# Sending the tokens of seven batches to their two experts through memory, in two waves, instead of running all eight experts on every token

## The reference, cut to what matters

```python
def _L3_ffn_ref(X, We, be, Wr, br, Wo, bo):
    router_logits = jnp.einsum('bsd,ed->bse', X, Wr) + br
    router_weights = jax.nn.softmax(router_logits, axis=-1)
    top_k_weights, top_k_indices = jax.lax.top_k(router_weights, TOP_K)
    expert_outputs = jnp.einsum('bsd,ehd->bseh', X, We) + be
    gathered = jnp.take_along_axis(expert_outputs, top_k_indices[..., None], axis=2)
    combined = jnp.sum(top_k_weights[..., None] * gathered, axis=2)
    out = jnp.einsum('bsd,hd->bsh', combined, Wo) + bo
    return out
```

## Time and profile before

| | us |
|---|---|
| median of 3 runs (652.51 to 654.73) | 654.12 |
| the profiled execution's own time | 654.19 |
| its span | 652.4 |
| PE busy in the span | 570.7 (87%) |
| DVE busy | 475.4 (73%) |
| ACT busy | 300.3 (46%) |
| POOL busy | 118.6 (18%) |
| mean granted PE clock | 0.97 of 2.4 GHz |

### The profile page before, as it was taken

How to read it: one execution, slowest core, us unless ns; L and a number is a source line. 1 busy time by engine, 2 the same in 40 slices (tenths; PEclk the granted TensorE clock), 3 DMA queues, 4 the chain that set the end, 5 groups by cost and what they waited for, 6 DMA issues and landing times.

```text
span 652.4 us, 10840 instructions
## 1 busy us (share of the span) xinstructions
PE 570.7 (87%) x3994; PEld 385.1 (59%) x4032; DVE 475.4 (73%) x1273; ACT 300.3 (46%) x472; POOL 118.6 (18%) x115
## 2 busy tenths in 40 slices
PE   9884776867989989989889888999999999999897
PEld 4743433745766756757667666656575756565443
DVE  4677868857678687787876776786968778786664
ACT  2346677626555455554545554243343425253110
POOL 2121000351313313313223132103030200000000
PEclk9886899889999999999999998999999999999999
DMA  9600000574135043143143240405032140000000
GB/s 335 258 1 1 1 0 2 127 220 128 52 98 150 28 123 114 56 132 113 35 146 89 59 146 19 127 1 162 2 100 62 41 122 16 2 17 1 17 18 16
DMA packets 40636, 51.15 MB, mean 78 GB/s; under 512 B 4180, under 2 KB 33620, under 8 KB 40276
## 3 DMA queue, kind: packets, MB, share of 16 engines
q1 hardware_dynamic: 40584, 50.46, 25.8%
HBM read 35.63 MB, written 14.68 MB: 77 GB/s over the span
## 4 chain that ended last, share of the span: by engine, by line
PE 50%; DVE 24%; issue 3%; DMA 1%; SPq 1%; ACT 1%; POOL 1%; DVEq 0%; ACTq 0%
PE ps L1317 13%; PE ps L1204 8%; PE ps L1196 7%; DVE nmax L1466 7%; PE ps L1279 4%; PE ps L1267 3%; PE ps L1247 3%; DVE xn L1422 2%; PE ps L1263 2%; PE ps L1188 2%; DVE stats L1411 2%; DVE acc L1551 2%; PE ps L1286 2%; PE ps L1242 2%; PE ps L1239 1%
## 5 line engine op out<-in xcount | busy, mean ns | idle before, releaser
L1466 DVE TENSOR_REDUCE nmax<-ps 128x2 f32<-128x512 f32 (+1 forms) x192 | 130.5, 681 | 70.5 <-PE ps L1247 67.7
L1368 ACT ACTIVATE PT<-ps 128x512 f32<-128x512 f32 x192 | 114.0, 597 | 145.3 <-PE ps L1267 143.2
L1317 PE MATMUL ps<-wm,xnT 128*128 128x512 f32 x256 | 120.1, 600 | 0.0
L1362 ACT ACTIVATE QS<-ps 8x1024 bf16<-8x1024 f32 x64 | 65.0, 1016 | 31.3 <-PE ps L1252 30.1
L1267 PE MATMUL ps<-QS,KS 110*128 110x256 bf16 (+3 forms) x512 | 75.0, 248 | 0.0
L1551 DVE SCALAR_TENSOR_TENSOR acc<-ps,gate,acc 128x256 f32<-128x256 f32 x128 | 61.6, 481 | 16.5 <-PE ps L1317 14.2
L1317 PEld LDWEIGHTS ps<-wm,xnT 128*128 128x128 f32 x256 | 44.6, 190 | 38.3 <-issue 38.0
L1263 PE MATMUL ps<-fixb 128*128 128x256 bf16 (+1 forms) x192 | 60.2, 314 | 7.5 <-DVE nmax L1466 3.5
L1148 POOL TENSOR_TENSOR rstd<-ve,fix 128x2 f32<-128x2 f32 x31 | 21.5, 693 | 247.9 <-DVE ve L1417 247.9
L1196 PE MATMUL ps<-xnT,by_dim 128*128 128x256 f32 x256 | 62.6, 390 | 2.2 <-ACT xnT L1333 2.2
L1168 POOL TENSOR_TENSOR parts<-rest,fix 128x512 bf16<-128x512 f32 x30 | 38.0, 1268 | 139.1 <-DVE rest L1435 100.5
(11 more groups left out here) (217 smaller groups left out, 882.8 us busy)
## 6 DMA issues: line engine op xcount, KB each, us to landing
parts_dram<-parts SPq DMA_DIRECT2D x32, 384.0 KB, 3.1
QS<-parts_dram SPq DMA_DIRECT2D x96, 128.0 KB
KS<-parts_dram SPq DMA_DIRECT2D x96, 128.0 KB, 2.6
wt<-wt_dram SPq DMA_DIRECT2D x1, 2562.0 KB, 19.2
wm<-wm_dram SPq DMA_DIRECT2D x1, 2449.0 KB, 13.0
xc<-x_dram SPq DMA_DIRECT2D x8, 256.0 KB, 5.3
out_dram<-res SPq DMA_DIRECT2D x8, 256.0 KB, 2.1
w<-w_dram SPq DMA_DIRECT2D x1, 845.0 KB, 7.5
```

What stands on the lines that cost most here:

```text
L1317: mm = pe.matmul(d, normT(stage, batch)[:, c, t * P:(t + 1) * P], M("We", c * EXPERTS * CH + e * 2 * CH, 2 * CH), start=(c == 0), stop=(c ...
L1362: act.activation(QS[MAX_AT:MAX_AT + MAX_ROWS, stack(stage, batch), 4 * n:4 * n + 4, :], bank(piece)[MAX_AT:MAX_AT + MAX_ROWS, 0:PIX].unsqu ...
L1368: act.activation(PT[:, pt_slot(piece, n), :], bank(piece), ACT.Exp).then_inc(drain(piece), 1)
L1466: dve.tensor_reduce(group[:, 0, :] if part == 0 else group[:, 1, 2 * part - 2:2 * part], bank(piece).rearrange("p (j n) -> p j n", n=w_), ...
```

## The change

Batches 0 to 3 are the first wave, batches 4 to 6 the second. For a sent batch the E pieces are gone. Instead:

- RT 3 also keeps the two picks and their gates apart (`mask`, `gains`). RK (step 31) counts on PE, by small bf16 products with a triangle of ones, how many earlier tokens of the wave chose each expert. SL (32) makes of that a row number for each token and pick (`slots`): each expert owns a region of a DRAM tensor `by_expert`.
- SC (32) sends the normalised tokens `xn` there: four indirect DMAs of 128 rows of 1 KB per batch, issued by POOL. LNb of the next batch, which overwrites `xn`, waits for them on DVE (`rows_sent`).
- BL, after the wave's last batch, makes a list of 128-row blocks and their experts: some fourteen small DVE operations. The number of blocks is a bound, not what the router chose: 24 (12 pairs) in the first wave and 20 (10 pairs) in the second. Blocks over the real number run on rows that hold zeros.
- For each pair of blocks: BD loads both from DRAM on SP, each after loading a register with its row; BT transposes them on PE (four transposes) and ACT copies them; BY loads a register with the expert, twice, and multiplies (four products 256 columns wide, 8 instructions), and ACT copies; BS stores both to their places on SP.
- GA gathers, for one batch at a time, each token's two results: four indirect DMAs on POOL, which wait for the wave's last stores. CB adds them to the residual with their gates: four DVE operations. CT follows.
- All rows of both DRAM tensors, 9216 and 7168 rows of 1 KB, are first filled with zeros by two DMAs from a zeroed part of `hp2` in the first half; DVE waits for them (`rows_zeroed`) before it first writes `hp2`.
- Batch 7 keeps its E pieces, four at steps 33 to 36 and four at 46 to 49.

```diff
+WAVES = ((0, 1, 2, 3), (4, 5, 6))
+SENT = sum(len(w) for w in WAVES)
+FIRST_PAIR = (38, 47)
+PAIR_STEP = (3, 1)
+PAIRS_IN, PAIRS_TURNED, PAIRS_OUT = 3, 2, 2
...
+def pairs(wave):
+    blocks = (2 * room(wave) + EXPERTS * (P - 1)) // P
+    return (blocks + 1) // 2
...
-        ("GB", 3, 0, 32), ("E", 3, 0, 35), ("E", 3, 1, 36), ("E", 3, 2, 37), ("E", 3, 3, 38), ("E", 3, 4, 39),
-        ("E", 3, 5, 40), ("E", 3, 6, 41), ("E", 3, 7, 42), ("CT", 3, 0, 44)),
+        ("GB", 3, 0, 32)),
 }
+DENSE_AT = {7: (33, 34, 35, 36, 46, 47, 48, 49)}
+def dense(batch):
+    at = DENSE_AT[batch]
+    return tuple(("E", 3, n, at[n]) for n in range(EXPERTS)) + (("CT", 3, 0, at[-1] + 6),)
+def flow(stage, batch):
+    if stage == 0 or batch >= SENT:
+        return FLOW[stage] + (dense(batch) if stage else ())
+    wave = wave_of(batch)
+    out, last = list(FLOW[stage]), WAVES[wave][-1]
+    out += [("RK", 3, 0, 31), ("SL", 3, 0, 32), ("SC", 3, 0, 32)]
+    start, apart = FIRST_PAIR[wave], PAIR_STEP[wave]
+    end = start + apart * pairs(wave) + 2
+    if batch == last:
+        out.append(("BL", 3, 0, 32))
+        for k in range(pairs(wave)):
+            at = start + apart * k
+            out += [("BD", 3, k, at - 3), ("BT", 3, k, at), ("BY", 3, k, at + 1), ("BS", 3, k, at + 1)]
+    at = end + BODY * (last - batch) + (batch - WAVES[wave][0])
+    out += [("GA", 3, 0, at), ("CB", 3, 0, at + 1), ("CT", 3, 0, at + 2)]
+    return tuple(out)
...
+                sp.wait_ge(padded_zero, 2)
+                sp.wait_ge(wt_loaded, 16)
+                zeros = hp2[:].rearrange("p b h w -> p (b h w)")[:, 0:8 * CH].bitcast(F32)
+                for w, rows in enumerate(by_expert):
+                    sp.dma_start(rows.rearrange("(p a r) n -> p a (r n)", p=P, r=4),
+                                 zeros.unsqueeze(1).broadcast_to([P, all_rows(w) // P // 4, 4 * CH])).then_inc(rows_zeroed, 16)
...
+                    if k == 2:
+                        dve.wait_ge(rows_zeroed, 16 * len(WAVES))
...
+                if kind == "BD":
+                    w = wave_of(batch)
+                    wait(sp, "blocks_ready", ("BL", stage, batch, 0))
+                    wait(sp, "rows_sent", ("SC", stage, batch, 0))
+                    if pair_before(piece, PAIRS_IN):
+                        full(sp, ("BT", *pair_before(piece, PAIRS_IN)))
+                    for j in range(2):
+                        k = 2 * n + j
+                        row_value[w, k] = sp.value_load(block_row[0:1, w, k:k + 1], min_val=0, max_val=all_rows(w) - P)
+                        sp.dma_start(rows_in[:, pair_at(piece, PAIRS_IN), j], by_expert[w][bass.ds(row_value[w, k], P), :])\
+                            .then_inc(sems[f"block_loaded{pair_at(piece, PAIRS_IN)}"], 16)
+                if kind == "BS":
+                    w = wave_of(batch)
+                    drained(sp, ("BY", stage, batch, n))
+                    for j in range(2):
+                        sp.dma_start(by_expert[w][bass.ds(row_value[w, 2 * n + j], P), :], rows_out[:, pair_at(piece, PAIRS_OUT), j])\
+                            .then_inc(sems[f"block_stored{pair_at(piece, PAIRS_OUT)}"], 16)
...
+                if kind == "SC":
+                    wait(pool, "slots_ready", ("SL", stage, batch, 0))
+                    for k in range(2):
+                        for t in range(2):
+                            pool.indirect_dma_start(by_expert[wave_of(batch)][:, :],
+                                                    bass.IndirectOffsetOnAxis(slots[:, batch, k, t:t + 1], 0),
+                                                    xn[:, 1, t, :], None).then_inc(sems["rows_sent"], 16)
+                if kind == "GA":
+                    w = wave_of(batch)
+                    for k in range(PAIRS_OUT):
+                        sent = ("BS", stage, WAVES[w][-1], pairs(w) - 1 - k)
+                        wait(pool, f"block_stored{pair_at(sent, PAIRS_OUT)}", sent)
+                    wait(pool, "combined", before(("CB", stage, batch, 0), 2))
+                    for k in range(2):
+                        for t in range(2):
+                            pool.indirect_dma_start(fetched[:, par, t, k, :], None, by_expert[w][:, :],
+                                                    bass.IndirectOffsetOnAxis(slots[:, batch, k, t:t + 1], 0))\
+                                .then_inc(sems[f"rows_fetched{par}"], 16)
...
+                if kind == "BT":
+                    wait(pe, f"block_loaded{pair_at(piece, PAIRS_IN)}", ("BD", stage, batch, n))
+                    src = rows_in[:, pair_at(piece, PAIRS_IN)]
+                    for j in range(2):
+                        for c in range(NC2):
+                            mm = pe.transpose(d[:, (j * NC2 + c) * P:(j * NC2 + c + 1) * P], src[:, j, c * P:(c + 1) * P],
+                                              F("ident"))
+                if kind == "BY":
+                    w = wave_of(batch)
+                    drained(pe, ("BT", stage, batch, n))
+                    wait(pe, "blocks_ready", ("BL", stage, batch, 0))
+                    for j in range(2):
+                        k = 2 * n + j
+                        at = pe.value_load(block_expert[0:1, w, k:k + 1], min_val=0, max_val=(EXPERTS - 1) * CH)
+                        for c in range(NC2):
+                            weights = M("We", c * EXPERTS * CH, EXPERTS * CH)
+                            mm = pe.matmul(d[:, j * CH:(j + 1) * CH], turned_in[:, pair_at(piece, PAIRS_TURNED), j, c, :],
+                                           weights[:, bass.ds(at, CH)], start=(c == 0), stop=(c == 1))
                 if kind == "CT":
-                    drained(pe, ("E", stage, batch, 7))
-                    drained(pe, ("E", stage, batch, 3))
-                    mm = turn4(acc)
+                    if batch < SENT:
+                        wait(pe, "combined", ("CB", stage, batch, 0))
+                    else:
+                        drained(pe, ("E", stage, batch, 7))
+                        drained(pe, ("E", stage, batch, 3))
+                    mm = turn4(X[:, 2 * batch:2 * batch + 2, :])
...
+                    if stage == 3 and 0 < batch <= SENT:
+                        wait(dve, "rows_sent", ("SC", stage, batch - 1, 0))
...
+                if kind == "CB":
+                    wait(dve, f"rows_fetched{par}", ("GA", stage, batch, 0))
+                    for k in range(2):
+                        for t in range(2):
+                            into = X[:, 2 * batch + t, :]
+                            op = dve.scalar_tensor_tensor(into, fetched[:, par, t, k, :], gains[:, batch, k, t:t + 1], into,
+                                                          ALU.mult, ALU.add)
+                        if k == 0:
+                            settle(op)
+                    op.then_inc(sems["combined"], 1)
```

More of the change, by code:

```diff
@@ L255, in build @@
         wo_loaded = sem("wo_loaded")
+        rows_zeroed = sem("rows_zeroed")
+        by_expert = [nc.dram_tensor(f"by_expert{w}_dram", (all_rows(w), CH), F32, kind="Internal").ap()
+                      for w in range(len(WAVES))]
         wm_loaded = sem("wm_loaded")
```

176 lines of the change are left out of this document (160 added, 16 removed).

## The result

The changed kernel takes **714.94 us** (median of 4 runs, 712.02 to 716.19) against 653.32 (650.49 to 654.73) for the kernel before, run beside it: ratio 1.0943, 95% interval 1.0891 to 1.0994, 61.6 us slower. The profiled execution took 714.48 us, its span is 712.7, the granted clock 0.917. The forecast was 694, slower.

A forecast was written before the change was run, and what follows sets the result against it. PE bounds the stretches with E pieces; without them the chain PE, DVE, ACT, PE bounds a body. From 654.2 us, bodies -30 and tail +69 gave 694 us, range 645 to 740.

The forecast's parts named there:

- the tail: After the last body: one chain of pairs, stores, gathers and combinations, 109.7 us instead of 40.33, +69 us.
- signs of being right: Bodies 10 to 12 about 30 us, PE idle at four CTs, ten pairs 4 us apart, last stretch over 100 us.
- What bounds the bodies: Bodies 10 to 12 without E pieces: the chain PE, DVE, ACT, PE bounds them, 91.2 us for 113.0, -21.8.
- the stretch of 29.20: Earlier profile, 375.50 to 404.70: attention and a router, no E piece, PE busy 23.85 us; the model for bodies.
- Rival 1: Whole kernel: PE's work sets the pace everywhere, 654 - 50 = 604 us; chance 0.08.
- SC at nothing: Sends on POOL: SPLIT delayed 4.8 us without harm, no DVE wait unless a send costs over 1.7 us.
- BL at nothing: Block list before the first wave's pairs: only something BD on SP waits for, no time charged.
- The second pair: Stretch of body 13: three pairs at 2.6 us each, no load wait counted; body 15's loads stand behind BD.
- Pairs in the bodies: Bodies 13 to 15: 2.6 us a pair; 4.1 if cover goes, 16 us over eleven pairs.
- Single prices: Terms of the tail: gather 1.2 us, pair 4.1, store landing 2.1, register load 0.6.
- rivals 2 and 3: Whole kernel: every price at its low end, 648 us, chance 0.08; gathers about 2.6 us each, 733 us, chance 0.12.
- Fill: Zero fill in the first half: ends between 67 and 91 us, taken as 0, at the other end +5 us.

The follow-up runs named there:

- bare: Changed kernel without the sends, block products, gathers and combination, with rank, slot and block arithmetic kept: 620.66 us.
- ring: Changed kernel with the sends at step 36.5 behind SPLIT, two xn buffers for stage 3, first wave's pairs two steps later: 703.41 us.
- no_send: Changed kernel without the 28 indirect DMAs that send the rows and the waits for them: 706.11 us.
- both repairs: Against ring (late sends, second xn buffer), the first wave's pairs moved three more steps later, from 40 to 43: 690.94 us.

## Why the prediction was right, and where its terms were off

The forecast loss was 40 us and the measured one 61.6. The direction and the tail came as forecast, and the 21 us that were missing lie in the bodies; of the signs of being right that the prediction named, the first one, stretches of about 30 us in bodies 10 to 12, didn't come.

- **What bounds the bodies.** Right, and the heart of it: without E pieces a body costs what its chain costs, 30.4 us as taken from the stretch of 29.20. Bare has 30.75 and ring 30.81 in body 10. Rival 1 (PE's work sets the pace, 604) is out: without any expert work for seven batches the kernel takes 620.7.
- **SC at nothing.** This term failed. "DVE doesn't wait unless a send costs over 1.7 us": a send costs 1.26, and that wait indeed isn't there. But "SC delays SPLIT on POOL by 4.8 us, and SPLIT has over ten steps until its scores" looked at SPLIT's own reader, and not at what else runs beside SPLIT where it lands. Measured by no_send: 10.7 us in bodies 10 to 13, 9.2 with body 9.
- **BL at nothing.** The sum has seven more DVE operations a body, and BL only as something that SP waits for. Its fourteen small operations stand in DVE's chain at the end of bodies 12 and 15. In body 12 bare has 33.62 us for the forecast 30.4, without a send or a pair.
- **The second pair.** "Three in the stretch of body 13" at 2.6 us each had no load to wait for, and the loads of body 15 were said to stand behind BD. They stand behind the first BD, but ahead of the second. The second BT stood 5.04 us for its block, and 2.44 without the sends.
- **Pairs in the bodies.** The prediction named the price if their cover goes, 4.1 us and not 2.6. In body 15, 28.4 us for 24.3, it does go in part: three BYs wait 4.2 us together for their copies. BL's operations stand there too, from 599.22 to 602.00, ahead of the last `attn`; the two were not told apart.
- **The sum of the misses.** 21.4 us over bodies 9 to 15: 6.6 in bodies 10 and 11, where ring takes all but 0.9 of them away; 6.7 in body 12, of which bare still has 3.2; 5.2 in body 13; 4.1 in body 15; -1.2 in 9 and 14. With both repairs the changed kernel takes 690.9 us. That this lies next to 694 is in part luck: its bodies take 211.5 us for the 206.6 forecast, with two pairs fewer in them, and its tail 103.6 for 109.7, with two more.
- **The tail.** Right, link by link. From its start, forecast and measured: copy of the wave's last pair done 7.2 and 7.0; first gather 10.2 and 9.5; CB of batch 0 done 19.0 and 18.0; CT of batch 3 34 and 35.4; first BY done 44 and 45.1; last BY 81 and 81.6; second gathers from 84.6 and 84.7; all issued 99.0 and 99.8; end 109.7 and 110.3.
- **Single prices.** A gather 1.2, measured 0.96 + 0.30 = 1.26; a pair 4.1, measured 4.06; a store's landing 2.1, measured 1.8; a register load on PE 0.6, measured 0.30, and 0.17 for the register arithmetic and the check of bounds behind it. So rivals 2 and 3 (all cheap, gathers dear at 2.6) are out. The Trainium skill, "DMA: Bandwidth & Descriptors", section on the anatomy of a DMA on the GpSimd path, has making the descriptors as a small part of such a DMA. No row shows how much of POOL's time that is; line 1310 has POOL busy 0.96 us for each gather, beside a landing of 2.8, so POOL's own part is no small one here.
- **Fill.** Nothing, as taken.

## What to carry to other kernels

Work taken from the engine that the span calls busy is worth only what the chain under it lets go: run the kernel once with the new work left out (here 620.7 of 652.4) before building it. What the sends cost was what stood behind them, so put sends behind every operation that another engine waits for in that queue, and give the rows they read a buffer of their own. Small operations that look like nothing (BL, 2.9 us) count in full where a chain runs through their engine. In a tail where one engine's order is fixed, a wait for gathers stops everything behind it; order by when things arrive.
